# The two applies of each memory head: key tiles 0 and 1 as three passes of halves, tiles 3 and 2 first in plain fp32

## What is computed

```python
keys, values = split(ss @ w_kv)              # chunks of 64 tokens
grads = vmap(grad(chunk_loss))(mem_ws, keys, lr, values)
momentum = assoc_scan(gm, -grads)
updates  = assoc_scan(gd, momentum)
w0, w1 = mem_w0 + updates[0], mem_w1 + updates[1]
x    = einsum('bhncd,bhnde->bhnce', q, w0)
vals = einsum('bhncd,bhnde->bhnce', silu(x), w1)
vals = rmsnorm(vals) * (mh_gamma + 1.0) * gate
out  = vals.reshape(...) @ w_combine
```

## Time and profile before

| | |
|---|---|
| median of 3 runs | 1116.36 us (1113.86 to 1116.4) |
| profiled execution | 1116.89 us, its span 1115.1 us |
| TensorE busy | 1073.0 us, 96% of the span |
| VectorE, ScalarE, GpSimd busy | 678.8, 677.0, 561.4 us |
| mean granted TensorE clock | 0.988 |

### The profile page before, as it was taken

One profiled execution on the slowest core, in us unless ns is written; L12 is line 12 of the kernel. 1 busy time (PEld: TensorE's weight loads), 2 busy tenths in 40 slices (PEclk: granted clock), 3 DMA queues, 4 the chain that ended last, 5 costly groups with the idle time before them and its releaser, 6 DMA issues. The chain is left out here.

```text
span 1115.1 us, 19052 instructions
## 1 busy us (share of the span) xinstructions
PE 1073.0 (96%) x6613; PEld 900.3 (81%) x6613; DVE 678.8 (61%) x1752; ACT 677.0 (61%) x1356; POOL 561.4 (50%) x574
## 2 busy tenths in 40 slices
PE   6999799999999999999999999999999999999994
PEld 4666588888888888888888888888888888888783
DVE  5887566766765555565555555565556555566664
ACT  5776366666655656565556655565656555566663
POOL 6885244478874444344534444344434454444453
PEclk9999699999999999999999999999999999999998
DMA  7210300000030000000000000000000000011221
GB/s 204 81 44 29 104 1 1 1 15 30 20 96 14 19 10 9 8 21 10 9 11 9 19 11 8 9 20 11 8 8 11 20 10 6 3 53 49 69 69 42
DMA packets 42129, 32.66 MB, mean 29 GB/s; under 512 B 4042, under 2 KB 36652, under 8 KB 41900
## 3 DMA queue, kind: packets, MB, share of 16 engines
q1 hardware_dynamic: 38484, 25.93, 8.1%
q0 software_dynamic: 2304, 4.74, 1.3%
q10 hardware_dynamic: 1248, 0.79, 0.2%
HBM read 18.30 MB, written 13.41 MB: 28 GB/s over the span
## 5 line engine op out<-in xcount | busy, mean ns | idle before, releaser
L1040 DVE TENSOR_TENSOR p_sb<-bank,coef 128x512 f32<-128x512 f32 (+3 forms) x512 | 218.7, 483 | 3.1 <-PE bank L749 2.6
L1232 POOL TENSOR_TENSOR sq_rest<-sq,sq_high 128x450 f32<-128x450 f32 x64 | 67.0, 1048 | 243.7 <-ACT sq_high L934 243.7
L772 PE MATMUL bank<-p_sb,du_t 128*128 128x450 f32 (+3 forms) x512 | 130.1, 397 | 4.4 <-ACT du_t L950 4.4
L772 PE MATMUL bank<-p_sb,err_t 128*128 128x450 f32 (+3 forms) x512 | 132.9, 402 | 0.2 <-DVE p_sb L1040 0.2
L772 PEld LDWEIGHTS bank<-p_sb,du_t 128*128 128x128 f32 x512 | 82.1, 190 | 48.9 <-issue 23.9
L772 PEld LDWEIGHTS bank<-p_sb,err_t 128*128 128x128 f32 x512 | 83.7, 190 | 45.6 <-DVE p_sb L1040 25.2
L1236 POOL TENSOR_TENSOR sq_low<-sq_rest,sq_mid 128x450 bf16<-128x450 f32 x64 | 67.5, 1054 | 104.3 <-ACT sq_mid L953 104.1
L1093 DVE SCALAR_TENSOR_TENSOR acc<-bank,rg,acc 128x128 f32<-128x128 f32 x224 | 62.8, 343 | 68.0 <-POOL rg L1220 68.0
L903 ACT ACTIVATE xs<-bank 128x450 f32<-128x450 f32 x64 | 35.0, 547 | 107.4 <-PE bank L772 107.4
L1118 DVE SCALAR_TENSOR_TENSOR du<-q_sb,bank 128x512 f32<-128x512 f32 x64 | 44.1, 689 | 89.0 <-PE bank L749 89.0
L1216 POOL TENSOR_TENSOR rs<-ms,neg_half 128x4 f32<-128x4 f32 x64 | 80.5, 1258 | 28.2 <-DVE ms L1075 26.8
(11 more groups left out here) (297 smaller groups left out, 3094.5 us busy)
## 6 DMA issues: line engine op xcount, KB each, us to landing
sorted_rows<-coef SPq DMA_DIRECT2D x5, 516.0 KB, 5.0
rows<-sorted_rows SPq DMA_DIRECT2D x40, 64.5 KB, 1.8
x<-in_L_attn_inputs SPq DMA_DIRECT2D x8, 256.0 KB, 5.5
x_rows<-x SPq DMA_DIRECT2D x8, 256.0 KB, 2.3
ew<-in_L_ffn_w SPq DMA_DIRECT2D x8, 256.0 KB, 4.0
attn_out<-acc SPq DMA_DIRECT2D x7, 256.0 KB, 2.1
ew<-attn_out SPq DMA_DIRECT2D x7, 256.0 KB
ew<-ffn_rows SPq DMA_DIRECT2D x8, 192.0 KB
```

The source lines that it names most:

```text
L772: last = pe.matmul(out[:, P * i:QW], rows[:, i, :], p_sb[:, P_COL[i]:P_COL[i] + QW - P * i], start=False, stop=True, skip_group_check=True)
L1040: last = nc.vector.tensor_tensor(dst, src, w, ALU.mult)
L1232: nc.gpsimd.tensor_tensor(sq_rest[:], sq[:], sq_3[0][:], ALU.subtract).then_inc(g_rest, 1)
```

## The change

In both applies the tiles 3 and 2 come first, as plain fp32, once all of `p_sb` is there (`made` at 3n + 3). Tiles 0 and 1 follow, each as three fp32r matmuls: high rows and low rows with the high part of `p_sb`, then high rows with its low part. For that, the high part of `p_sb` for tiles 0 and 1 is cast on ScalarE (`p_high_of`, 450 and 322 columns) and the low part subtracted on VectorE (`p_low_of`), twice a head; `err_t` and `du_t` hold only tiles 2 and 3, and the rows of tiles 0 and 1 are made as `err_t2` and `du_t2` in halves: `err_t` goes through `th`, its high part on ScalarE, its low part on GpSimd (`g_el`); `du_t` has its high part on ScalarE and its low part on VectorE. On VectorE `err_low` moves ahead of both `q_sb`. On ScalarE the block's rows move ahead of `err_t`, and `gate_rows`/`scale_rows` are split in two, half behind `err_high` and half behind `sq_mid`. Some buffers are shared: `du` is `err`, `sq_rest` is `sq`, `token_q` and `per_token` lie in `amd`.

```diff
-                def apply(out, rows, made, n):
-                    for i in SC_ORDER:
-                        if i != 3:
-                            pe.wait_ge(made, SC_BANKS * n + {0: 1, 1: 2, 2: 3}[i])
-                        last = pe.matmul(out[:, P * i:QW], rows[:, i, :], p_sb[:, P_COL[i]:P_COL[i] + QW - P * i],
-                                         start=False, stop=True, skip_group_check=True)
+                def apply(out, plain, halves, made, n, high, low, lows):
+
+                    pe.wait_ge(made, SC_BANKS * n + 3)
+                    for i in (3, 2):
+                        pe.matmul(out[:, P * i:QW], plain[:, i - 2, :], p_sb[:, P_COL[i]:P_COL[i] + QW - P * i],
+                                  start=False, stop=True, skip_group_check=True)
+                    for i in (0, 1):
+                        cols = QW - P * i
+                        p_high, p_low = (part[:, QW * i:QW * i + cols] for part in p_2)
+                        pe.wait_ge(high, 2 * n + i + 1)
+                        pe.wait_ge(low, lows * n + lows - 2)
+                        for rows in halves:
+                            pe.matmul(out[:, P * i:QW], rows[:, i, :], p_high, start=False, stop=True, skip_group_check=True)
+                        pe.wait_ge(low, lows * n + lows - 1 + i)
+                        last = pe.matmul(out[:, P * i:QW], halves[0][:, i, :], p_low, start=False, stop=True, skip_group_check=True)
                     return last
...
+                def p_high_of(made, n, i, done):
+
+                    cols = QW - P * i
+                    act.wait_ge(made, SC_BANKS * n + i + 1)
+                    nc.scalar.copy(p_2[0][:, QW * i:QW * i + cols], p_sb[:, P_COL[i]:P_COL[i] + cols]).then_inc(done, 1)
...
+                    if s is not None:
+                        p_high_of(v_p1, k, 0, a_p1)
+                        p_high_of(v_p1, k, 1, a_p1)
+                    if f is not None:
                         act.wait_ge(p_e, n + 1)
                         act.wait_ge(p_d, n)
                         nc.scalar.copy(err[:], EB[:]).then_inc(a_err, 1)
...
                     if f is not None:
+                        act.wait_ge(p_et, n + 1)
+                        act.wait_ge(v_g, n + 1)
+                        nc.scalar.copy(th[:, 0:2 * D], XB[:, 0:2 * D])
+                        nc.scalar.copy(err_t[:].rearrange("p t d -> p (t d)"), XB[:, 2 * D:]).then_inc(a_et, 1)
+                        p_high_of(v_p0, n, 0, a_p0)
                         act.wait_ge(p_dt, n + 1)
-                        nc.scalar.copy(du_t[:].rearrange("p t d -> p (t d)"), EB[:]).then_inc(a_dt, 1)
+                        nc.scalar.copy(du_t2[0][:].rearrange("p t d -> p (t d)"), EB[:, 0:2 * D])
+                        nc.scalar.copy(du_t[:].rearrange("p t d -> p (t d)"), EB[:, 2 * D:]).then_inc(a_dt, 1)
+                        p_high_of(v_p0, n, 1, a_p0)
+                        act.wait_ge(a_et, 2 * n + 1)
+                        nc.scalar.copy(err_t2[0][:].rearrange("p t d -> p (t d)"), th[:, 0:2 * D]).then_inc(a_et, 1)
...
                     if s is not None:
                         dve.wait_ge(p_x, k + 1)
                         weigh(s, p_s1, v_p1, k)
+                        p_low_of(a_p1, k, 0, v_l1)
+                        p_low_of(a_p1, k, 1, v_l1)
                     if f is not None:
+                        dve.wait_ge(a_eh, n + 1)
+                        nc.vector.tensor_tensor(err_2[1][:], err[:], err_2[0][:], ALU.subtract).then_inc(v_el, 1)
...
                         weigh(f, p_s0, v_p0, n, s)
+                        dve.wait_ge(a_dt, n + 1)
+                        nc.vector.tensor_tensor(du_t2[1][:].rearrange("p t d -> p (t d)"), EB[:, 0:2 * D],
+                                                du_t2[0][:].rearrange("p t d -> p (t d)"), ALU.subtract).then_inc(v_l0, 1)
+                        p_low_of(a_p0, n, 0, v_l0)
+                        p_low_of(a_p0, n, 1, v_l0)
...
+                    if f is not None:
+                        pool.wait_ge(a_et, 2 * n + 2)
+                        flat = [part[:].rearrange("p t d -> p (t d)") for part in err_t2]
+                        nc.gpsimd.tensor_tensor(flat[1], th[:, 0:2 * D], flat[0], ALU.subtract).then_inc(g_el, 1)
```

77 lines of the change are left out of this document (42 added, 35 removed).

## The result

The changed kernel takes 1189.6 us (median of 4 runs, 1188.15 to 1190.5), beside 1116.24 for the kernel before: a ratio of 1.066, with an interval of 1.065 to 1.068. It is slower, as forecast, but by 73 us and not by 41, and the time lies above the range. Its profiled span is 1186.3 us. From here on a step is read from the start of the product E to the next E (the last step, which has no E behind it, to the last product of xs and w1).

| stage, E to E | before | forecast | after |
|---|---|---|---|
| 17 steps, batches 0 and 1 | 238.3 | +14 | 268.5 (+30) |
| 40 block steps | 629.3 | +25 | 661.0 (+32) |
| 7 steps, the last plain ones | 100.8 | +2.5 | 112.0 (+11) |

What follows compares the result with a forecast made beforehand. The prediction took TensorE, busy 96% of the span, as the bound. Its terms, 25 + 2 + 0 + 3.7 + 8 + 2.5 = +41 us, took the profiled 1116.9 to 1158, or 1157 from the runs' median; range 1122 to 1182.

Steps and rivals of the forecast that it cites:

- It starts at about 511.6: First apply of a block step: TensorE must wait for all of p_sb, at 511.53 instead of starting at 510.58.
- So an apply has 1.07 in place of 1.29: Tiles 0 and 1 of each apply on TensorE: three fp32r passes save 0.22 us, about 1.5 us with small tiles.
- I leave both out of the sum: VectorE contention with GpSimd: 4 us more by one row or 12 by the rule, kept only in the range.
- block steps, 40: First apply ends 0.55 us later, second apply's chain delays too: each block step +0.6 us, +25 in all.
- plain with nothing else, 4: Plain steps: first apply gains 0.22, q_sb wait costs 0.3, second apply ends about 0.45 later: +2 us.
- scale only, 5: Steps that only scale rows: splitting the rows takes away the delay of the du copy: 0.
- indirect DMAs only, 3: GpSimd: later sq_mid and the new 0.80 us operation start rs 1.2 us late: +3.7 us over three steps.
- indirect DMAs and `starts`, 5: GpSimd without slack before rs: 0.8 for sq_mid and 0.8 for the new operation, +1.6 each, +8 us.
- last seven: Last batch: row split and applies give time back, but GpSimd's 0.94 us idleness is used up: +0.35 each, +2.5.
- TensorE as the bound throughout: Rival: other engines never hold TensorE, 28 us less, 1088, up to 1110 with some waits; chance 0.11.
- only the first wait counts: Rival: second apply finds its halves ready and GpSimd keeps slack; 40 x 0.3, about 1123; chance 0.20.
- The third: Rival: GpSimd's chain moves in block steps too, or contention slows it, 0.5 us more each, 1177; chance 0.15.

Runs made afterwards that it cites:

- e1: Kernel before with both applies waiting for all of p_sb and taking tiles 3, 2, 0, 1, all plain fp32: 1168.16 us, ratio 1.0477.
- e7: Kernel before with VectorE's last-batch row sums waiting for ScalarE's sq_mid, so laid beside GpSimd's sq_low and product: 1121.42 us, ratio 1.0041.
- e13: Changed kernel with GpSimd's errt_low cut to 2 of 256 columns from the third head on: 1179.8 us, ratio 1.0566 to the kernel before.
- e8: Changed kernel with VectorE's last_sum and add_rows moved behind xs_low of the next step: 1186.03 us, ratio 1.0621 to the kernel before.
- e14: Changed kernel with errt_low cut to 2 columns and VectorE's closing sums and row adds moved behind xs_low: 1176.24 us, ratio 1.0537 to the kernel before.
- e3: Kernel before with only ScalarE's gate_rows and scale_rows split in two parts: 1110.32 us, ratio 0.9933.
- e15: Changed kernel with VectorE's table work (scans, block counts, row places) moved behind xs_low of the next step: 1196.16 us, ratio 1.0709 to the kernel before.
- e5: Changed kernel with only the second apply (du_t) in halves, the first plain again: 1135.82 us, ratio 1.0170 to the kernel before.
- e6: Changed kernel with only the first apply (err_t) in halves, the second plain again: 1170.16 us, ratio 1.0479 to the kernel before.
- e9: Changed kernel with VectorE's err_low put back behind both copies of q_sb: 1198.68 us, ratio 1.0722 to the kernel before.

## Why the prediction was right or wrong

**Right: the sign and the main wait.** "It starts at about 511.6" was E + 2.43; it is E + 2.41. The wait forecast as 0.9 us is 0.86, and e1 shows it as the cost of taking all of `p_sb` first. The second apply was put at E + 8.78 and starts at E + 8.92.

**Mis-sized: "So an apply has 1.07 in place of 1.29 ... about 1.5 us from start to end".** It is 1.71 and 1.75. The 0.22 us itself was nearly right: against e1, the same order in plain fp32, the halves save 0.24 and 0.17. Two things were wrong in the 1.5. Of 0.44 to 0.55 us for the small tiles I had reckoned with the low end, and the starts give 0.55. And I had written "1.5 long in place of 1.95 (the old one lost time following the weighing)"; e1's apply follows nothing and is 1.95 long. The extra 0.10 us stands at the first record of the apply, in the old order too: there the next starts 0.48 us behind it, and 0.38 in the second apply (510.58 to 511.06, 517.19 to 517.56). In e1 and in the changed kernel it is 0.16 (695.84 to 696.00), where a 66-column record inside the old apply has 0.06 (518.48 to 518.54). So 1.07 + 0.55 + 0.10 = 1.72. Against the old second apply (1.84), which had no such extra, the gain is 0.09 us, where 1.5 would have been 0.34. The first apply ends 0.19 us later than I wrote (E + 4.12, not E + 3.93), and what follows in the step shifts with it. The second then ends at E + 10.67 and not E + 10.48: the step is +0.8 and not +0.6. That length is the whole miss of the block steps, 31.7 us for 25.

**Failed: "I leave both out of the sum".** The row that I bounded contention with, 0.79 against 0.61 us, had only 0.29 us of overlap with GpSimd (239.84 to 240.13). I took its 0.18 us as the most that a link could lose. It was 0.18 of 0.29, and with longer overlaps `xs_low` lost 1.44, a `p_low` pair 0.85, four row sums 2.3 us. The kernel before had a better row, a VectorE scan beside GpSimd's `sq_low`:

```profile
306.68 1.47 DVE L987 TENSOR_TENSOR_SCAN coef<-ew 128x256 f32<-128x256 f32 x1
```

```profile
306.54 1.05 POOL L1236 TENSOR_TENSOR sq_low<-sq_rest,sq_mid 128x450 bf16<-128x450 f32 x1
```

It takes 0.69 us with no such operation beside it (315.97 in the changed kernel), so it lost 0.78 us in 0.91 us of overlap. The 12 us of the other bound would also have grown `du_low`, which reads one of its two inputs from a PSUM bank; it took 0.42 us, as reckoned without contention. The GPSIMD Engine Reference of the Trainium skill (section 8, Key points) has the two engines sharing SBUF interfaces, with contention for VectorE instructions that have two SBUF inputs; the trace agrees, and e7 and e13 show it with 371 to 784 ns and 2.05 to 1.53 us. I had also looked for it in the wrong steps: in block steps, which show none of it, and not where GpSimd is full.

**Failed: the plain steps.** Term by term, in the steps' own lengths:

| term | forecast | measured |
|---|---|---|
| block steps, 40 | +25 | +31.7 |
| plain with nothing else, 4 | +2 | +4.8 (3.1 of it in the first step) |
| scale only, 5 | 0 | +8.4 (3.4 of it in the step with the placing of rows) |
| indirect DMAs only, 3 | +3.7 | +4.9 |
| indirect DMAs and `starts`, 5 | +8 | +12.2 |
| last seven | +2.5 | +11.2 |

I had followed TensorE, ScalarE and GpSimd there, and VectorE only up to `p_low`. Behind `p_low` stand the closing sums, the scans and, once each, the block counts and the places of rows, and `ms` and `xs_low` stand behind those. In the kernel before all of that fitted under TensorE. Of the last seven steps' 11.2 us, e8 gives 5.5 back by VectorE's order alone, e13 4.0 and e14 8.7: "+2.5" was GpSimd's share, and VectorE's was left out. The +11.2 is also net of the rows' split: against e3 the halves lose 16.1 us there. Of the 30 us in the 17 steps, e13 gives back 6.5 (in part because the wait of 2.17 us is 1.69 there and the clock does not fall behind it) and e8 none, and e15 makes them worse. What is left is split over the two applies by e5 and e6 (12 and 17), and rows show it as many waits of 0.2 to 0.5 us (`p_low`, `q_sb`, `xs_low`, `s_low`). Which of these would remain if one were taken away was not run, except for `errt_low` and the tables; that part stays open.

**Right in kind:** the wait for `q_sb` in plain steps, forecast as 0.3 each, measured as 9.5 us in 23 places. e9 shows that the change's order keeps it small.

**The rivals.** TensorE as the bound throughout (1088) fell with e1; "only the first wait counts" was right of the block steps, where e5 shows the second apply at +0.06 us and e6 the first at +0.73; its 0.3 was less than half of that. The third (1172 to 1190, contention) holds the time, by its second name and in other steps than it says. The buffers, put at nothing, cost at most 0.2% where tried; the rows' split, credited with 0.57 us a step in the last batch, is worth 0.84.

## What to carry to other kernels

An order that lets a consumer start on the first tile can be worth more than the arithmetic: waiting for all of it cost 1.22 us a step, and the cheaper passes gave 0.41 of that back. Before moving work to an engine with 39% of its time free, walk that engine's whole step, with whatever stands behind the added work in the steps that have something extra, and ask who waits for it. And scale a contention by the overlap in the row that shows it, not by the row's stretch.

## What the runs showed of the hardware

Two things I had not expected. First, a VectorE subtraction of two SBUF tiles almost stops for as long as GpSimd works on two SBUF inputs: `xs_low` got through some 0.05 of its 0.61 us in the 1.49 us beside `errt_low` and `ew`. The row sums got on a little: 0.42 of their 3.44 us lie outside GpSimd's three operations, and they need 1.13. Where VectorE's scans and GpSimd's two operations met in e15, both were stretched (0.69 to 1.11 and 0.79 to 1.24 us), so the loss can fall on either side. GpSimd's `rs`, which works on 128x4, did not slow it: `xs_low` takes 0.61 us with `rs` beside it (1149.38 and 1149.53 in the changed kernel). My reading of e15's rows is that the two take turns, an instruction at a time: `xs_low` ends at 306.12, `errt_low` at 306.71, the first scan at 307.32, `ew` at 307.92 and the second scan at 308.47, each 0.55 to 0.61 us behind the one before it on the other engine. Who starts first does not settle it: in the changed kernel `xs_low` starts 0.07 us ahead of `errt_low` and still lets both of GpSimd's go by. No run tested this further.

Second, a long wait can cost TensorE twice. In the changed kernel `ms` came late once behind the placing of rows; TensorE's timeline, and then three windows (us, busy time and instructions of the five engines, PEclk, DMA share, GB/s):

```profile
220.23 0.48 PE L749 MATMUL bank<-y_high,w_qk_high 128*128 128x450 f32 x1 [2.17 <-DVE ms L1116]
...
221.06 0.58 PE L749 MATMUL bank<-xs_high,s_high 128*128 128x450 f32 x1
221.43 0.58 PE L749 MATMUL bank<-xs_low,s_high 128*128 128x450 f32 x1
```

```profile
218.00:221.00 3.00, 0.83 (x4) 0.72 (x4) 2.54 (x12) 1.11 (x2) 0.74 (x1) 0.97 0.00 0
221.00:224.50 3.50, 3.50 (x13) 3.31 (x13) 2.61 (x8) 1.83 (x4) 3.12 (x4) 0.54 0.00 0
224.50:228.00 3.50, 3.41 (x21) 3.01 (x20) 2.82 (x6) 2.81 (x7) 0.00 (x0) 1.00 0.00 0
```

Two passes of 450 columns start 0.37 us apart there, and 0.20 apart elsewhere. The granted clock was 0.97, then 0.54 of full speed for 3.5 us (for most of it the lower level, 1.2 GHz), then 1.00 (2.4 GHz). The three wide and three narrow passes of that product took 222.99 - 221.06 = 1.93 us, where by 0.20 and 0.15 us each they take 1.05: some 0.9 us on top of the 2.17 us of waiting. The waits of up to 1.03 us from 240 to 340 us in the changed kernel left the clock at 1.00, and e15's of 1.88 us did not. Its length alone does not settle it: a wait of 2.29 us (for `xs_low`, before 143.43) and e13's of 1.69 left the clock at 1.00 too.
